# A written table of task slots for a fused attention and mixture-of-experts layer on one core

## The reference, cut to what matters

```
q, k, v = xn @ Wq.T, xn @ Wk.T, xn @ Wv.T            # 16 heads of 16
scores  = q @ k.T / 4                                 # causal, 1024 x 1024 per head
std     = softmax(scores) @ v @ Wo.T
gauss, dirp = exp(-0.5*|x-pos|^2/scale^2), tanh((x-pos).dir)   # 8 splats a head, of q and of k
splat   = (amp*qg) @ kg.T + 0.4 * (amp*qg*qd) @ (kg*kd).T
gsa     = softmax(scores + 0.3 * splat) @ v @ Wo.T
attn    = (1 - blend) * std + blend * gsa
experts = top-2 of 16 (gate sqrt(softplus)), capacity 128, plus one shared expert
          each expert: silu(x @ W1.T) * (x @ W3.T) @ W2.T, with an inner width of 176
```

## Time and profile before

| | us |
|---|---|
| median of 3 runs (lowest, highest) | 357.77 (357.11, 359.34) |
| the profiled execution's own time | 356.44 |
| its span, first to last instruction | 354.7 |
| mean granted TensorE clock in the span | 0.981 of 2.4 GHz |

### The profile page before, as it was taken

How to read it: one execution, slowest core, us unless ns; L and a number is a source line. 1 busy time by engine, 2 the same in 40 slices (tenths; PEclk the granted TensorE clock), 3 DMA queues, 4 the chain that set the end, 5 groups by cost and what they waited for, 6 DMA issues and landing times.

```text
span 354.7 us, 6091 instructions
## 1 busy us (share of the span) xinstructions
PE 316.1 (89%) x2064; PEld 161.2 (45%) x2064; DVE 235.8 (66%) x735; ACT 201.4 (57%) x300; POOL 39.7 (11%) x59
## 2 busy tenths in 40 slices
PE   0899898977779999999999999999999999999984
PEld 0548533223423455444544455445445554445352
DVE  4858776499997568964766567665766568666424
ACT  1696277575645576654565465555555545647730
POOL 7300000000020000111111111102110004444000
PEclk9998998999978999999999999999999999999999
DMA  7424353224146303635455536554554443222011
GB/s 243 132 43 65 57 99 88 55 43 67 30 65 167 73 2 48 137 112 138 112 140 116 161 87 146 129 143 100 128 145 134 102 80 78 59 72 60 7 59 59
DMA packets 25790, 33.54 MB, mean 95 GB/s; under 512 B 4636, under 2 KB 18556, under 8 KB 25756
## 3 DMA queue, kind: packets, MB, share of 16 engines
q1 hardware_dynamic: 24056, 28.85, 35.3%
q0 software_dynamic: 1536, 4.20, 4.3%
q10 hardware_dynamic: 164, 0.07, 0.1%
HBM read 16.15 MB, written 4.26 MB: 58 GB/s over the span
## 4 chain that ended last, share of the span: by engine, by line
PE 44%; DVE 5%; ACT 2%; issue 2%; DMA 1%; SPq 1%; DVEq 0%
PE ps L897 12%; PE ps L813 6%; PE ps L822 5%; PE ps L879 5%; PE ps L867 4%; PE ps L775 4%; PE ps L852 2%; DMA stage<-split 1%; PE ps L817 1%; PE ps L870 1%; ACT arena_p L670 1%; DVE mx L1215 1%; ACT small L682 1%; PE ps L826 1%; PE ps L801 1%
## 5 line engine op out<-in xcount | busy, mean ns | idle before, releaser
L670 ACT ACTIVATE arena_p<-ps 128x1024 f32<-128x1024 f32 (+1 forms) x192 | 148.0, 808 | 49.6 <-PE ps L879 29.2
L897 PE MATMUL ps<-arena_p,v_full 128*32 128x512 f32 (+3 forms) x768 | 72.6, 496 | 0.0
L1183 DVE CUSTOM_DVE_ANT_0 ps<-ps,mask_r 128x128 f32<-128x128 f32 (+3 forms) x128 | 61.7, 501 | 11.6 <-PE ps L775 6.9
L775 PE MATMUL ps<-stage 96*128 96x512 bf16 (+3 forms) x160 | 50.6, 354 | 8.1 <-DVE mx L1215 3.7
L867 PE MATMUL ps<-stage 98*128 98x512 bf16 (+1 forms) x192 | 51.6, 333 | 3.7 <-ACT arena_p L670 3.0
L1215 DVE TENSOR_REDUCE mx<-ps 128x1 f32<-128x512 f32 x64 | 43.9, 686 | 14.5 <-PE ps L775 14.1
L879 PE MATMUL ps<-stage 98*128 98x512 bf16 (+1 forms) x192 | 47.2, 334 | 2.5 <-ACT arena_p L670 2.3
L452 POOL DMA_INDIRECT wt<-xn_scratch,ids_sb x16 | 15.3, 954 | 235.3 <-PE ps L801 107.6
L897 PEld LDWEIGHTS ps<-arena_p,v_full 128*32 128x32 f32 x768 | 20.1, 110 | 34.6 <-issue 30.0
L775 PEld LDWEIGHTS ps<-stage 96*128 96x128 bf16 x160 | 15.6, 99 | 29.6 <-issue 22.2
L675 ACT ACTIVATE small<-ps 128x176 f32<-128x176 f32 x24 | 7.6, 317 | 37.2 <-PE ps L813 37.2
(11 more groups left out here) (199 smaller groups left out, 374.2 us busy)
## 6 DMA issues: line engine op xcount, KB each, us to landing
w_sb<-in_w_dram SPq DMA_DIRECT2D x16, 352.0 KB
stage<-split SPq DMA_DIRECT2D x48, 96.0 KB
stage<-split SPq DMA_DIRECT2D x96, 32.0 KB
stage<-split SPq DMA_DIRECT2D x48, 64.0 KB
arena_o<-in_w_dram SPq DMA_DIRECT2D x16, 176.0 KB
ye_scratch<-wt SPq DMA_DIRECT2D x16, 128.0 KB, 2.6
stage<-split SPq DMA_DIRECT2D x32, 48.0 KB
acc<-in_x_dram SPq DMA_DIRECT2D x2, 512.0 KB, 4.7
```

What stands on the lines that cost most here:

```text
L670: A(to, ps[:, 1 + 2 * s:3 + 2 * s, off:CH], ACT.Exp, scale=SCALE).then_inc(done, 1)
L775: ins = M(b[:, 0:n1 - n0], qs[0:KR, pr, h, it * P:(it + 1) * P], ks[0:KR, pr, h, n0:n1], start=True, stop=True)
L897: ins = M(ps[c:c + 2 * HD, 0, off:CH], v_full[:, jb + s, g * GH + h, :], of, start=jb + s == 0, stop=end or last, skip_group_check=last an ...
L1183: return V.tensor_tensor_reduce(row, row, mask_r[:, CH - row.shape[1]:CH], 1.0, NEG, ALU.add, ALU.max, to)
```

## The change

Before, lists of tasks were spread evenly over ranges of slots (`spread`, `spread_late`), chains of an expert were put at fixed distances (`chain`), and every group from 1 to 6 had the same places for its maxima. After, `PLAN` is a literal: for each of the 8 groups, 24 lists of tasks, in the order in which every queue takes them. The tasks are the same, and none is computed otherwise. Two tasks go to an earlier group (`rest` 4 and 5, from group 1 to group 0) and two to a later one (`add` (1, 2) and (0, 3), from 6 to 7). `AT` is derived from the table. The prologue, the units, the number of banks and the end list are as they were.

```diff
-        maxima = spread_late(max0, 0, 6) + [(9, ("shift", 0))] + spread_late(max1, 7, 20) + [(22, ("shift", 1))]
-        first_rest = [(n // 2, ("pre", t)) for n, t in enumerate(max1[LATER:])] + [(4, ("pre", ("shift", 1)))]
-        first_maxima = spread_late(max0, 5, 9) + [(12, ("shift", 0))] + spread_late(max1, 10, 20) + [(22, ("shift", 1))]
-        HALF = [(2, ("square", 0)), (3, ("square", 1)),
-                (4, ("feat1", (0, 1))), (5, ("feat1", (1, 1))), (6, ("feat1", (0, 0))), (7, ("feat1", (1, 0))),
-                (8, ("p0", 4)), (9, ("p0", 5)), (24, ("rest", 4)), (26, ("rest", 5)), (28, ("p1", 4)), (30, ("p1", 5)),
...
-        EXPERT = ((("xT", 0), ("gu", 2), ("hT", 5), ("y", 6)), (("xT", 5), ("gu", 7), ("hT", 9), ("y", 10)))
...
+        PLAN = [
+            [
+                [("pre", ("max", (1, 4, 0))), ("pre", ("max", (1, 4, 1))), ("pre", ("max", (1, 5, 0))),
+                 ("pre", ("max", (1, 5, 1)))],
+                [("pre", ("max", (1, 6, 0))), ("pre", ("max", (1, 6, 1))), ("pre", ("max", (1, 7, 0)))],
+                [("pre", ("max", (1, 7, 1)))],
+                [("max2", (0,))],
+                [("square", 0), ("square", 1), ("pre", ("shift", 1))],
+                [("max2", (1,)), ("p0", 4), ("max", (0, 2, 0))],
+                [("feat1", (0, 1)), ("feat1", (1, 1)), ("max", (0, 3, 0))],
+                [("max", (1, 2, 0))],
+                [("max", (1, 3, 0)), ("route", 0)],
+                [("p0", 5)],
+                [("max", (0, 4, 0)), ("feat1", (0, 0)), ("feat1", (1, 0)), ("max", (0, 4, 1)), ("max", (0, 5, 0)),
+                 ("max", (0, 5, 1))],
+                [("route", 1), ("oT", 0)],
...
+                [("max", (1, 7, 0)), ("max", (1, 7, 1)), ("rest", 4)],
+                [("route", 4)],
+                [],
+                [("shift", 1)],
+                [("route", 5), ("rest", 5)],
...
```

Group 3 after, which stands for groups 2 to 5; before, `shift` 0 stood at slot 9, `max` (0, 5, 0) and (0, 5, 1) at 9, (0, 6, 1) and (0, 7, 0) behind `oT` at 11, `xT` 6 at slot 20 and both `max2` behind `hT` 2 and `xT` 3 at slot 1:

```diff
+                [],
+                [("hT", 2), ("xT", 3), ("oT", 1)],
+                [("y", 2), ("max2", (0,))],
+                [("gu", 3), ("max2", (1,)), ("max", (0, 2, 0))],
...
+                [("shift", 0)],
+                [("xT", 4), ("max", (0, 5, 0))],
+                [("max", (0, 5, 1)), ("max", (0, 6, 0))],
+                [("oT", 0), ("gu", 4), ("max", (0, 6, 1))],
+                [("max", (0, 7, 0)), ("max", (0, 7, 1))],
+                [("hT", 4)],
...
+                [("hT", 5), ("max", (1, 6, 0))],
+                [("y", 5), ("xT", 6), ("max", (1, 6, 1))],
```

More of the change, by code:

```diff
@@ L229, in bass_splat_attention_moe_layer @@
         max1 = [("max", (h, it, pc)) for h in range(GH) for it in range(TC, NT) for pc in range(2)]
-        def slotted(*lists):
-            slots = [[] for _ in range(NSLOT)]
-            for entries in lists:
-                for at, t in entries:
-                    slots[at].append(t)
-            return slots
         ROUTE = 8
         CUM, IDS = 4, 7
-        def spread_late(tasks, first, last):
-            late_slots = [n for n in range(first, last + 1) if n % 4]
-            return [(late_slots[len(late_slots) * n // len(tasks)], t) for n, t in enumerate(tasks)]
@@ L247, in spread @@
-        def spread(tasks, first, last):
-            return [(first + (last + 1 - first) * n // len(tasks), t) for n, t in enumerate(tasks)]
-        def chain(steps, count, at, period):
-            return [(at + period * (n // 2) + slot, (kind, n)) for n in range(count) for kind, slot in steps[n % 2]]
-        SHARED = ((("sgu", 2), ("shT", 5), ("sy", 6)), (("sgu", 7), ("shT", 9), ("sy", 10)))
-        EXPERT = ((("xT", 0), ("gu", 2), ("hT", 5), ("y", 6)), (("xT", 5), ("gu", 7), ("hT", 9), ("y", 10)))
@@ L256, in bass_splat_attention_moe_layer @@
-        maxima = spread_late(max0, 0, 6) + [(9, ("shift", 0))] + spread_late(max1, 7, 20) + [(22, ("shift", 1))]
-        LATER = 8
-        first_rest = [(n // 2, ("pre", t)) for n, t in enumerate(max1[LATER:])] + [(4, ("pre", ("shift", 1)))]
-        first_maxima = spread_late(max0, 5, 9) + [(12, ("shift", 0))] + spread_late(max1, 10, 20) + [(22, ("shift", 1))]
-        HALF = [(2, ("square", 0)), (3, ("square", 1)),
-                (4, ("feat1", (0, 1))), (5, ("feat1", (1, 1))), (6, ("feat1", (0, 0))), (7, ("feat1", (1, 0))),
-                (8, ("p0", 4)), (9, ("p0", 5)), (24, ("rest", 4)), (26, ("rest", 5)), (28, ("p1", 4)), (30, ("p1", 5)),
-                (34, ("third", 4)), (37, ("third", 5)), (42, ("product", 1)), (44, ("p0", 6)), (46, ("p0", 7)),
-                (48, ("rest", 6)), (50, ("rest", 7)), (52, ("p1", 6)), (55, ("p1", 7)), (58, ("third", 6)), (62, ("third", 7))]
+        LATER = 8
@@ L268, in bass_splat_attention_moe_layer @@
         LAST_FEAT = ("feat1", (1, 0))
-        S_ROUTE, S_SHARED, S_EXPERT, S_ADD = (8, 31), (32, 148), 56, 156
         OWN_AT = (0, 3)
-        long = HALF + spread([("route", k) for k in range(ROUTE)], *S_ROUTE)
-        for half in range(2):
-            long += [(at, (kind, n + half * NT // 2)) for at, (kind, n) in chain(SHARED, NT // 2, S_SHARED[half], 12)]
-        long += [(S_EXPERT - 24 + 5 * e, ("weights", e)) for e in range(WB - 1)]
-        long += chain(EXPERT, E, S_EXPERT, 12)
-        long += spread([("add", (k, n)) for n in range(NT) for k in range(2)], S_ADD, 7 * NSLOT + 16)
@@ L295, in bass_splat_attention_moe_layer @@
+        AT = {t: g * NSLOT + n for g, slots in enumerate(PLAN) for n, tasks in enumerate(slots) for t in tasks
+              if t[0] not in ("max2", "max", "shift", "pre", "oT")}
         END = [("rowsh", 0), ("oTh", 1), ("out", (TC, 1)), ("rowsh", 1), ("out", (TC + 2, 1))]
```

196 lines of the change are left out of this document (180 added, 16 removed).

## The result

The changed kernel takes 343.69 us (median of 4 runs, 343.12 to 344.20), the kernel before 358.29 (median of 4, 357.11 to 359.34): a ratio of 0.9593, with an interval of 0.9556 to 0.963. That is 14.6 us less (the 357.77 of the forecast was the median of the first three runs of the kernel before; a fourth is in the 358.29). The forecast was 6.8 less, 351.0, and its range ended at 346.5. The profiled execution took 343.12 us with a span of 341.3 and a mean clock of 0.988.

The account below looks back on a forecast made before the run. VectorE was taken to bound the stretch from group 0 to 1, TensorE the steady groups. Terms -2.4 - 0.3 + 0.2 + 0 - 3.8 - 0.5 = -6.8 us gave 351.0 us, range 346.5 to 356.0.

Parts of the forecast that it names:

- The term for the waits: Groups 1 to 6: TensorE's waits mostly removed by reordering, -3.8 us; -0.6 in group 1, -0.8 each in 2 to 5, 0 in 6.
- the VectorE stretch: Slot 8 of group 0 to that of group 1: VectorE sets the pace and keeps its work, +0.2 us.
- the clock: 103.4 to 109.0 us: the half-clock episode, costing 2.8 us, stays at this size; term 0, bounds -2.8 and +2.8.
- Slots 4 to 9: Group 0: two long `feat1`, 3.74 us together, move to slot 10 under VectorE's work; -2.4 us, bounds -3.7 and 0.
- ScalarE's passes: Group 0, slots 4 to 7: squares and `p0` 4 put ahead of exponentials make TensorE wait, 1.3 us taken off the gain.
- Slots 0 to 3: Group 0: four maxima in slot 0 run while TensorE waits for the first exponential; -0.3 us, bounds -1.0 and +0.4.
- its absence: Rival: the clock episode in the VectorE stretch goes as well, 348.2 us; chance 0.18.
- the six waits of the steady group: Six visible TensorE waits, 1.36 us together: five go, 1.08 us visible plus about 0.07 each; `y` behind `hT` stays.
- the 0.3 for `std` behind a `splat` exponential: Steady group: with `gu` moved from slot 10 to 11, `std` waits for ScalarE's exponential; 0.3 us lost.
- The rival of bursts: Slots with three to five maxima overrun three PSUM banks and TensorE waits: 10.8 us more, 361.8 us; chance 0.10.
- The last group: `out` (0, 2) moves behind both `splat`, covering a 0.79 us `std` wait; the 0.98 at the end stays; -0.5 us.
- the signs of being wrong: VectorE stretch grows by the start's gain, L1215 and L1183 waits exceed 7 us in groups 1 to 6, or a second clock fall.

Follow-up runs that it names:

- e9: Kernel before with both long `feat1` in slot 10 of group 0, both `square` in slot 4 and `p0` 4 in slot 5: 357.17 us, 0.9991.
- e3: Kernel before with groups 2 to 4 from the new table: 349.96 us, 0.9775.
- e12: Kernel before with only group 1 from the new table, `rest` 4 and 5 in its slots 0 and 2: 355.23 us, 0.9975.
- e2: Kernel before with only `feat1` (0, 0) and (1, 0) moved from slots 6 and 7 to slot 10 of group 0: 355.47 us, 0.9945.
- e4: Kernel before with groups 5 to 7 from the new table: 358.73 us, 1.0039.
- e8: Kernel before with slots 8 to 12 of groups 2 to 5 in the order of the new group 3: 353.69 us, 0.9883.
- e15: Kernel before with only slots 10 to 23 of group 0 from the new table, `feat1` left in slots 6 and 7: 354.46 us, 0.9928.
- e5: Changed kernel with group 5 written like its group 3 and group 6 with at most two maxima per slot, `add` as before: 338.95 us, 0.948 to kernel before.
- e1: Kernel before with groups 0 and 1 from the new table: 348.54 us, 0.9728.
- e6: Changed kernel with group 6's five maxima of slot 5 spread over slots 5 to 7: 341.75 us, 0.9564 to the kernel before.
- e7: Changed kernel with `rest` 4 and 5 back in group 1: 341.70 us, 0.9572 to the kernel before.
- e14: Kernel before with all of group 0 from the new table: 348.75 us, 0.977.
- e10: Changed kernel with `feat1` (0, 0) and (1, 0) back in slots 6 and 7 of group 0: 346.70 us, 0.9699 to the kernel before.
- e11: Kernel before with slots 0 to 9 of group 0 from the new table and both long `feat1` in slot 10: 354.26 us, 0.9918.

## Why the prediction was too high

The direction was right, and the size was off by a factor of two. In the balance above 6.6 us lie between the forecast and the measured change. The term for the waits is too small by 5.3 in groups 1 to 4, which is the largest miss, and has the wrong sign in groups 5 and 6 (2.4 the other way); the start is too small by 1.9, the VectorE stretch by 1.6, the end by 0.2. So the steps that failed are the size of the waits term (-3.8 for groups 1 to 6, measured -6.7), the clock, which I had put at 0, and two sizes at the start.

**Slots 4 to 9, forecast -2.4: too small by 1.9.** From `pv` to `pv` it is 10.35 - 6.08 = 4.27 us. The move of the two `feat1` gives 3.44 in the old table and 3.37 in the new, nearly all of their 3.74. ScalarE's passes, for which I had taken 1.3 off, cost 0.95 among the old maxima (e9). What I hadn't seen is the third term: with `feat1` left where it was, the new order of the rest (the late maxima of the first group gone from slots 4 and 5, `max2` and the squares differently placed) still gives 0.90. So the passes' price was not far off by itself, and in the new table the other moves pay for it; what the passes cost there was not measured apart.

**Slots 0 to 3, forecast -0.3: too small by 1.1.** It is 6.69 - 5.32 = 1.37 us. Of this 0.84 is the order of the tasks (6.16 to 5.32, both without a fall), near the -1.0 that I had as the bound, and 0.53 a fall of the clock at 54 to 58 us. The 0.90 of the stretch in the earlier trace rows showed it, and I didn't ask for its place. This 0.53 is partly luck of the execution: with the old slots 0 to 3 the fall stands in three traces (before, e3, e12) and not in four others (e2, e4, e8, e15), with the new ones in none of nine. Against both terms stands the prologue, unchanged code, which took 1.0 us more in the profiled execution after than in that before (the first `std` starts at 52.05 to 53.16 us over all traces); so the balance has -4.64 and not -5.64.

**The VectorE stretch and its clock, forecast +0.2 and 0: too small by 1.6, and by the 1.0 of the fall that ran over into group 1.** This is the step that failed in kind. I had forecast that a fall of that size stays, and had given 0.18 to its absence. What happened is between: a fall stayed, of 3.5 us instead of 6.9, and stands where VectorE is full (2.90 of 3.00 us), so that it should cost little. One execution speaks for that: of the five of e5, which has the same group 0, four have a mean clock of 0.988 to 0.990 and took 338.33 to 339.26 us, and the one at 1.000, which can have had no fall in the prologue either, took 339.19. With slots 10 to 23 new, it went by whether `feat1` stood in slot 10: with it (the table after, e1, e5, e6, e7, e14) there is one short fall between 92 and 98 us, without it (e10, e15) there are two. Slots 0 to 9 alone (e11) gave 40.41 us for the stretch, more than before. So my treating the stretch as a constant that only moves was wrong in both directions. The clock can account for all that I missed here: the old fall has 4.9 us inside the stretch and 2.0 behind it, at half clock, and by the price of e4 and e8 it cost up to 2.4 and 1.0 us. That is an estimate; the order of the tasks changed with it, and how much of the 1.36 us is order and how much clock stays open. What places a fall also stays open, since some executions of unchanged code had one at 82 to 86 and others not.

**Groups 1 to 4 and the waits, forecast -3.0, measured -8.3 from slot 8 of group 1 to that of 5.** Of the six waits of the steady group the five that I had named are gone, and so is the sixth (0.28 us, `y` behind `hT`), which I had as staying; one of 0.2 is new. Three amounts were wrong. The sixth wait was not counted. A removed wait gives 0.13 us more than it shows, not 0.07 (e8). And the 0.3 for `std` behind a `splat` exponential and the 0.3 for unseen waits, together nearly half of the gross gain, were guesses: the one new wait of the steady group shows 0.2. Group 3 lost 1.66 us, its visible waits 1.36 - 0.2 = 1.16; the other 0.5 can be seen in TensorE's busy time, which fell from 34.91 to 34.38 us with the same matmuls, as it would if each wait uncovers the end of the matmul before it. Against the forecast of 0.8 that is 0.3 for the sixth wait, 0.2 for the price and 0.4 for the guesses. I had also taken one group for all: groups 1, 2 and 4 were 0.6 to 1.7 us longer than group 3 before, and gave more. Group 1's share contains 1.0 for the end of the clock's fall, so that some 7.3 of the 8.3 us are waits and what they uncover.

**Groups 5 and 6, forecast -0.8 and 0, measured +1.94 and -0.36.** I had let group 3 stand for groups 2 to 5, and it doesn't for group 5: with the experts' numbers moved, 22 of its 24 slots differ from group 3 (18 in group 2, 16 in group 4). `hT` 10 stands in slot 0, five maxima stand in slots 8 and 9. From slot 8 of group 5 to the `pv` ahead of slot 4 of group 6 the two traces need the same time, 29.94 and 29.93 us: nothing of the forecast 0.8 came. Written in the order of group 3 (e5), the stretch to slot 8 of group 6 is 35.71 us, 1.5 below before. The pair with the burst then costs 1.4 us more than the old one (7.40, before 5.99), and 0.5 lies in the late copy behind it, which two other traces of the same table don't have; there the stretch is 38.27 us, 1.1 above before and not 1.9. Taking the burst apart moved the loss further on (e6), so that it isn't the burst alone. The rival of bursts had its mechanism here, and of its 10.8 us between 1 and 2 came.

**The last group, -0.5, measured -0.69.** The `std` wait of 0.79 is gone, as forecast, and the wait at the very end grew from 0.98 to 1.11.

Of the signs of being wrong, one came in part: there is no second fall beside the one in the VectorE stretch where TensorE has work, but one in the last 1.5 us.

The Trainium skill (TensorE: Matmul & The Clock Gate, psum-queue depth-cycling) tells of a kernel that cycles through PSUM banks and whose frequent short idle times between groups of matmuls make the clock go back and forth between its two levels. From this I had the bursts bring a second fall. The granted clock in group 6 with its five maxima in a row was 1.00, so that this isn't borne out by the short waits here:

```profile
270.00:281.00 11.00, 10.34 (x73) 4.97 (x71) 6.55 (x24) 4.02 (x10) 1.33 (x2) 1.00 0.32 62
```

The falls whose approach I read stand behind stretches in which TensorE had longer to wait: busy for 1.23 of 3.40 us in the earlier trace rows, 0.48 of 2.00 in e11, and in the kernel after:

```profile
87.00:94.00 7.00, 4.72 (x46) 2.51 (x50) 6.76 (x27) 5.35 (x8) 0.00 (x0) 1.00 0.23 34
```
